# Layer 0 of the first two pairs entirely as squares of sums, and state copies by TensorE at the start

## What is computed

```python
e = stack([tbl_f[ids[:, f]] for f in range(32)], axis=1)      # 1024 x 32 x 16
x0, xk, outs = e, e, []
for W in (W0, W1, W2):                                        # W0 32x32x64, W1 and W2 32x64x64
    xk = relu(einsum('bmd,bhd,mhk->bkd', x0, xk, W))
    outs.append(sum(xk, axis=2))
h = concatenate([concatenate(outs, axis=1), dense_ctx], axis=1)
h = maximum(h @ W_top1 + b_top1, 0)
h = maximum(h @ W_top2 + b_top2, 0)
y = h @ W_top3
```

## Time and profile before

| | |
|---|---|
| median of 3 runs | 651.24 us (650.84 to 652.83) |
| the profiled execution | 651.33 us, its span 649.5 us |
| TensorE busy | 593.5 us (91%) |
| VectorE busy | 542.6 us (84%) |
| GpSimd busy | 441.0 us (68%) |
| ScalarE busy | 399.5 us (62%) |

### The profile page before, as it was taken

One profiled execution on the slowest core, in us unless ns is written; L12 is line 12 of the kernel. 1 busy time (PEld: TensorE's weight loads), 2 busy tenths in 40 slices (PEclk: granted clock), 3 DMA queues, 4 the chain that ended last, 5 costly groups with the idle time before them and its releaser, 6 DMA issues.

```text
span 649.5 us, 7363 instructions
## 1 busy us (share of the span) xinstructions
PE 593.5 (91%) x2580; PEld 187.3 (29%) x2580; DVE 542.6 (84%) x292; ACT 399.5 (62%) x644; POOL 441.0 (68%) x303
## 2 busy tenths in 40 slices
PE   0158699799999999999999999999999999999897
PEld 0012122233332333333333333333333333322243
DVE  0039889799899998989898989898999989899700
ACT  0041554967676777858586767676767778666032
POOL 5737766678897788889898988885989842522000
PEclk9998799999999999999999999999999999999999
DMA  3296989897978786959596968687877869030000
GB/s 102 70 248 145 225 190 235 205 221 194 216 197 193 207 181 182 207 157 214 144 213 169 196 168 200 150 213 149 211 167 197 179 188 194 32 64 0 9 9 0
DMA packets 41671, 104.57 MB, mean 161 GB/s; under 512 B 16897, under 2 KB 25665, under 8 KB 33442
## 3 DMA queue, kind: packets, MB, share of 16 engines
q1 hardware_dynamic: 32562, 100.53, 64.5%
q0 software_dynamic: 8192, 2.11, 3.6%
q10 hardware_dynamic: 880, 1.46, 0.8%
HBM read 99.08 MB, written 4.20 MB: 159 GB/s over the span
## 4 chain that ended last, share of the span: by engine, by line
PE 77%; DMA 7%; DVE 5%; issue 4%; POOL 4%; SPq 2%; ACT 1%; DVEq 0%
PE acc L531 59%; PE pair_sum L503 4%; DVE prod L330 4%; POOL gath L256 4%; PE pair_sum L518 4%; PE pair_sum L511 3%; DMA x_scratch<-gath 3%; PE pair_sum L524 2%; PE rep L589 2%; DMA gath<-in_tables,rows_sb 2%; DMA x_rot<-x_scratch 1%; SPq L231 1%; PE rep L581 1%; PE rep L582 1%; DVE z_sb L335 0%
## 5 line engine op out<-in xcount | busy, mean ns | idle before, releaser
L330 DVE TENSOR_TENSOR prod<-m_rep,rep 128x2048 f32<-128x2048 f32 x227 | 503.1, 2281 | 15.5 <-PE acc L531 11.2
L531 PE MATMUL acc<-prod,w_sb 128*64 128x512 f32 x1816 | 410.5, 601 | 18.4 <-DVE prod L330 16.5
L418 ACT COPY rep<-state 32x512 f32<-32x512 f32 x504 | 292.6, 581 | 52.2 <-DVE prod L330 45.3
L256 POOL DMA_INDIRECT gath<-in_tables,rows_sb x256 | 244.2, 954 | 94.8 <-issue 77.5
L531 PEld LDWEIGHTS acc<-prod,w_sb 128*64 128x64 f32 x1816 | 126.1, 138 | 295.9 <-issue 254.8
L267 POOL TENSOR_TENSOR prod_pool<-m_rep,xb 128x2048 f32<-128x2048 f32 x29 | 132.6, 4571 | 50.2 <-ACT xb L428 34.3
L267 POOL TENSOR_TENSOR prod_pool<-x_rot,x_rep 128x2048 f32<-128x2048 f32 x14 | 64.0, 4572 | 12.0 <-DMA x_rot<-x_scratch 9.0
L503 PE MATMUL pair_sum<-x0c,sel_sb 32*128 32x512 f32 x128 | 38.0, 670 | 26.7 <-DMA x0c<-x_scratch 25.5
L390 ACT ACTIVATE state<-pair_sum 128x512 f32<-128x512 f32 x16 | 9.6, 597 | 79.9 <-PE pair_sum L524 79.9
L531 PE MATMUL acc<-prod_pool,w_sb 128*64 128x512 f32 x232 | 54.7, 592 | 0.0
L411 ACT ACTIVATE sums_sq<-pair_sum 128x1024 f32<-128x1024 f32 x32 | 32.9, 1027 | 33.5 <-PE pair_sum L503 33.5
(11 more groups left out here) (27 smaller groups left out, 84.4 us busy)
## 6 DMA issues: line engine op xcount, KB each, us to landing
m_rep<-x_scratch SPq DMA_DIRECT2D x256, 256.0 KB, 9.4
x_rot<-x_scratch SPq DMA_DIRECT2D x32, 512.0 KB, 5.8
x_rep<-x_scratch SPq DMA_DIRECT2D x16, 512.0 KB, 3.8
gath<-in_tables,rows_sb POOLq DMA_INDIRECT x256
x_scratch<-gath SPq DMA_DIRECT2D x16, 256.0 KB
x0c<-x_scratch SPq DMA_DIRECT2D x32, 64.0 KB
w_sb<-in_w ACTq DMA_DIRECT2D x2, 512.0 KB, 4.6
m_rep<-z_sb SPq DMA_DIRECT2D x12, 64.0 KB, 2.3
```

The costliest lines, as they stand in the source:

```text
L256: pool.indirect_dma_start(out=gath[p % 2][:, g, :], out_offset=None, in_=tables, in_offset=bass.IndirectOffsetOnAxis(ap=rows_sb[:, n:n + 1 ...
L330: nc.vector.tensor_tensor(prod[:, number % RING], in0, in1[:, None, :].to_broadcast([128, 2, PAIR]), ALU.mult).then_inc(unit_ready, 1)
L418: last = nc.scalar.copy(rep[v][M * q:M * q + M, CHUNK * a:CHUNK * a + CHUNK], state[l - 1][K * a + M * v:K * a + M * v + M, :])
L531: last = nc.tensor.matmul(acc[K * a:K * a + K, :], w, src[:, k, CHUNK * a:CHUNK * a + CHUNK], start=start and k == 0, stop=stop and k == 1)
```

## The change

For pairs 0 and 1 (`EARLY = 2`) all four tiles of layer 0 are squares of sums, with the weights of tiles 0 and 1 halved (`half_sb`) and a diagonal of their own (`wdiag0_sb`). So `x_rep` and `x_rot` are not loaded for them, and the scratch is written once instead of twice. The gathered rows of a pair now lie as four blocks of 32 partitions, one for each quarter of the columns. Pair 0's sums are made straight from them by 16 matmuls of 256 columns, two pair-sum tiles at a time into eight PSUM half-tiles; pair 1's `x0c` is copied from them within the chip. TensorE runs five extra matmuls (`WARM`) once 10 gathers have landed. For slots 0 and 1, `rep[0]` of slot 2 and `rep[0]` of slot 3, the state is copied by matmuls with a 0/1 matrix (`copy_state`). Slot 0 takes its units in the order (0,0) (1,0) (0,1) (1,1) ... , which uses `m_rep` tiles as they land. On GpSimd `layer0_product(2)` comes after seven fours of gathers instead of eight.

```diff
 def order(i):
     if i == 0:
-        return [(0, 0), (0, 1), (1, 0), (1, 1), (0, 2), (1, 2), (0, 3), (1, 3)]
+        return [(v, u) for u in range(4) for v in range(2)]
...
 # SyncE, for p in range(NP)
-                sp.wait_ge(gathered[p % 2], 16 * GPP * (p // 2 + 1))
-                dst = x0_dram[p].rearrange("(again m) c -> again (m c)", again=2).rearrange("again (r c) -> r again c", c=PAIR // Q)
-                src = gath[p % 2][:, :, :].rearrange("r g d -> r (g d)")
-                sp.dma_start(dst, src[:, None, :].to_broadcast([128, 2, PAIR // Q])).then_inc(x0_stored, 16)
-                sp.wait_ge(x0_stored, 16 * (p + 1))
-                after(sp, l0_done, p - 1)
-                for a in range(2):
...
+                gathered_all(sp, p)
+                rows = gath[p % 2][:, :, :].rearrange("r g d -> r (g d)")
+                if p == 1:
+                    for q in range(Q):
+                        at = M * (q // 2), PAIR // Q * (q % 2)
+                        sp.dma_start(x0c[1][at[0]:at[0] + M, at[1]:at[1] + PAIR // Q],
+                                     rows[M * q:M * q + M, :]).then_inc(x0c_in[1], 16)
+                for again in range(1 if p < EARLY else 2):
+                    row = x0_dram[p, M * again:M * again + 1, :]
+                    dst = bass.AP(row.tensor, row.offset, [[PAIR // Q, Q], [PAIR, M], [1, PAIR // Q]])
+                    sp.dma_start(dst, rows).then_inc(x0_stored, 16)
+                sp.wait_ge(x0_stored, x0_stored_to(p + 1))
+                if p > 1:
+                    after(sp, l0_done, p - 1)
+                    for a in range(2):
+                        sp.dma_start(x0c[p % 2][M * a:M * a + M, :],
+                                     x0_dram[p, 0:M, CHUNK * a:CHUNK * a + CHUNK]).then_inc(x0c_in[p % 2], 16)
+                if p >= EARLY:
...
 # GpSimd
-            for n in range(8):
+            for n in range(7):
                 pool.wait_ge(unit_ready, 2 * n + 1)
                 gather(2 * GPP + 4 * n, 4)
             layer0_product(2)
-            for n in range(8, 10):
+            for n in range(7, 10):
...
 # VectorE
+            nc.vector.tensor_scalar(half_sb, w0_sb[:, 0:XT, :], 0.5, None, ALU.mult)
...
-            def first_layer0(p):
-                dve.wait_ge(x_in, 16 * (1 + XT) * (p + 1))
-                nc.vector.tensor_tensor(prod_pool[:, p], x_rot[:, :, :], x_rep[:, None, :].to_broadcast([128, XT, PAIR]),
-                                        ALU.mult).then_inc(first_x, 1)
...
-            def second_chunk(l):
...
 # ScalarE
-            square_x(0)
-            square(0, 0)
-            square(0, 1)
+            gathered_all(act, 0)
+            nc.scalar.activation(xsq[:, 0:PAIR // Q], gath[0][:, :, :].rearrange("r g d -> r (g d)"), SQUARE).then_inc(xsq_ready, 1)
+            act.wait_ge(first_sums, 1)
+            for half, sums in enumerate((pair_sum, rep[0])):
+                nc.scalar.activation(first_squares(0, half), by_block(sums), SQUARE).then_inc(first_sq, 1)
+            act.wait_ge(first_sums, 2)
+            nc.scalar.activation(first_squares(1, 0), by_block(rep[1]), SQUARE).then_inc(first_sq, 1)
+            for b, bank in enumerate((acc1, acc2)):
+                nc.scalar.activation(first_squares(1, 1)[:, b], bank[:, :].rearrange("p (t c) -> p t c", t=2),
+                                     SQUARE).then_inc(first_sq, 1)
             relu0(0)
-            replicate(0, 0, 1)
-            replicate(0, 1)
             relu_slot(0)
...
-                    square(i, 0)
-                    square(i, 1)
+                    for n in range(ST if i < EARLY else QB):
+                        square(i, n)
...
 # TensorE
+            def first_pair_sums():
+                gathered_all(pe, 0)
...
+                for sel_of, banks in ((sel0_sb, (pair_sum[:, 0:CHUNK], pair_sum[:, CHUNK:PAIR], rep[0][:, 0:CHUNK], rep[0][:, CHUNK:PAIR])),
+                                      (sel_sb, (rep[1][:, 0:CHUNK], rep[1][:, CHUNK:PAIR], acc1[:, :], acc2[:, :]))):
+                    for t in range(2):
+                        for q in range(Q):
+                            last = nc.tensor.matmul(banks[q][:, c * t:c * t + c], sel_of[M * q:M * q + M, t, :],
+                                                    rows[M * q:M * q + M, :], start=True, stop=True)
+                    last.then_inc(first_sums, 1)
...
+            def first_layer0():
+                pe.wait_ge(xsq_ready, 1)
+                pe.wait_ge(first_sq, 2)
+                layer0_tile(half_sb[:, 0, :], prod_pool[:, 0, 0, :], True, False)
+                first_diagonal(0)
+                layer0_tile(half_sb[:, 1, :], prod_pool[:, 0, 1, :], False, False)
+                first_diagonal(1)
+                pe.wait_ge(first_sq, 5)
+                for t in range(QB):
+                    last = layer0_tile(w0_sb[:, XT + t, :], sums_sq[:, t, :], False, t == QB - 1)
+                last.then_inc(l0_done, 1)
...
+            def copy_state(i, v):
+                l = SLOTS[i][0] - 1
+                pe.wait_ge(state_ready[l], SLOTS[i][1] + 1)
+                if i > 0:
+                    pe.wait_ge(unit_ready, UNIT_BASE[i] if i == 1 else UNIT_BASE[i - 1] + v0_units(i - 1))
+                for a in range(2):
+                    last = nc.tensor.matmul(rep[v][:, CHUNK * a:CHUNK * a + CHUNK], copies_sb[K * a:K * a + K, v, :],
+                                            state[l][K * a:K * a + K, :], start=True, stop=True)
+                last.then_inc(rep1_ready if v else rep0_ready, 1)
...
+            pe.wait_ge(first_gathered, 16 * WARM_FROM)
+            for _ in range(WARM):
+                nc.tensor.matmul(acc2[0:K, :], w_sb[1][:, 0, 0, :], w_sb[1][:, 0, :, :].rearrange("p t k -> p (t k)"),
+                                 start=True, stop=True)
+            first_pair_sums()
+            first_layer0()
+            copy_state(0, 0)
+            copy_state(0, 1)
...
+                    if i == 0 and n == 7:
+                        copy_state(1, 0)
+                        pair_sums(1, 0)
+                        copy_state(1, 1)
+                        pair_sums(1, 1)
+                    if i == 1 and n < 2:
+                        pair_sums(1, 2 + n)
+                    if i == 1 and n == 2:
+                        layer0_sums(1)
+                        layer0_rest(1)
+                    if i == 1 and n == 3:
+                        copy_state(2, 0)
...
+                    if (i, n) == (2, 3):
+                        layer0_sums(2)
+                    if (i, n) == (2, 4):
+                        layer0_rest(2)
+                    if (i, n) == (2, 5):
+                        copy_state(3, 0)
```

More of the change, by code:

```diff
@@ L211, in _ @@
-                for a in range(2):
[L212 to L215, removed]
-                rows = x0_dram[p, 0:1, :]
-                src = bass.AP(rows.tensor, rows.offset, [[PAIR, M], [0, Q], [1, PAIR]])
-                sp.dma_start(x_rep[:, :], src).then_inc(x_in, 16)
-                for t in range(XT):
-                    rows = x0_dram[p, 1 + Q * t:2 + Q * t, :]
-                    src = bass.AP(rows.tensor, rows.offset, [[PAIR, M], [PAIR, Q], [1, PAIR]])
-                    sp.dma_start(x_rot[:, t, :], src).then_inc(x_in, 16)
+                gathered_all(sp, p)
@@ new lines, in _ @@
+                sp.wait_ge(x0_stored, x0_stored_to(p + 1))
[5 more added lines that the diff above has]
+                if p >= EARLY:
+                    if p > EARLY:
+                        x_multiplied(sp, p - 1)
+                    row = x0_dram[p, 0:1, :]
+                    src = bass.AP(row.tensor, row.offset, [[PAIR, M], [0, Q], [1, PAIR]])
+                    sp.dma_start(x_rep[:, :], src).then_inc(x_in, 16)
+                    for t in range(XT):
+                        row = x0_dram[p, 1 + Q * t:2 + Q * t, :]
+                        src = bass.AP(row.tensor, row.offset, [[PAIR, M], [PAIR, Q], [1, PAIR]])
+                        sp.dma_start(x_rot[:, t, :], src).then_inc(x_in, 16)
@@ L336, in sum_d @@
                                         op=ALU.add, axis=AX_X).then_inc(z_ready[l], 1)
-            def second_chunk(l):
-                dve.wait_ge(state_ready[l], 1)
-                for q in range(Q):
-                    last = nc.vector.tensor_copy(rep[0][M * q:M * q + M, CHUNK:PAIR], state[l][K:K + M, :])
-                last.then_inc(first_rep, 1)
-                dve.wait_ge(first_rep, l + 1)
-            first_layer0(0)
             for i, (l, p) in enumerate(SLOTS):
                 base, nv = UNIT_BASE[i], v0_units(i)
-                if i < 2:
-                    second_chunk(i)
                 if i >= POOL_FROM:
@@ new lines, in layer0_tile, with first_diagonal @@
+            def layer0_tile(w, src, start, stop):
+                for a in range(2):
+                    last = nc.tensor.matmul(acc0[K * a:K * a + K, :], w, src[:, CHUNK * a:CHUNK * a + CHUNK],
```

(12 more changed lines are left out.)

178 lines of the change are left out of this document (105 added, 73 removed).

## The result

The changed kernel takes 649.93 us (median of 18 runs, 648.03 to 651.92), the kernel before 652.26 (18 runs, 650.45 to 654.36). The ratio is 0.9962, interval 0.9948 to 0.9976; the medians are 2.3 us apart. I had predicted 638.4 and a range that begins at 634.5 and ends at 643.5. The sign was right and most of the gain is missing. The profiled execution after has a span of 648.9 us against 649.5.

What follows compares the result with a forecast made beforehand. TensorE's own work bounds the middle, and a chain of DMA stages sets when it begins. That chain ends 12.9 us earlier (123.28 to 110.4), the engines' chain being ready at 108.0: 651.3 - 12.9 = 638.4 us, range 634.5 to 643.5.

Steps and rivals of the forecast that it cites:

- the DMA chain: Start, gathers, stores and loads of pairs 0 to 3: sets when the middle begins; 12.9 us earlier.
- 108.0: Engines' chain: TensorE ready for slot 3's pair sums at 108.0, 2.4 us before the data.
- taken two at a time: Pair 0's narrow matmuls: two overlap, so eight take 2.5 us; 1.3 if four overlap.
- 110.4: Slot 3's pair sums: start at 110.4 instead of 123.28, 2.3 us after x0c of pair 3 is issued.
- this moved step: GpSimd, pair 3's last four gathers behind layer0_product(2): landed at 103, at worst 106.5; costs nothing to 0.6 us.
- 2.15 us is nearly all latency: Pair 0's store, half as large: lands at 28.1 as before, no gain counted.
- The second store issue: Pair 2's stage: its 0.4 us is hidden, since the store waits behind the loads.
- my 51.2: Pair 1's gathers: the last lands at 51.2 instead of 58.3, bounds 46 and 53.
- the four `x0c` copies: Pair 1's stage on SyncE: four small issues before the store, 1.7 us in all.
- The next interval: From pair 1's stage at 55.1 to x0c of pair 2 at 78.8: 23.7 us instead of 31.2.
- I count full clock: TensorE in the start: no wait above about 2.3 us; otherwise 2 to 4 us more on the engines' chain.
- Rival A: Start: gathers land promptly, engines set the end at 108.0; 15.3 us less, 636.0 us; chance 0.14.
- Rival D: GpSimd: layer0_product(2), waiting for x_rot, delays pair 3's gathers; harm from x_rot at about 106, 655 at 110; chance 0.02.

Runs made afterwards that it cites:

- `f_best` paced: Changed kernel with pair 3's last gathers before GpSimd's product, stores as four DMAs, pair 1's store before its x0c copies, and pacing: 642.08 us (0.9860).
- the paced one: Changed kernel with SyncE waiting for each set of four m_rep loads before issuing the fourth of the next: 648.64 us (0.9957).
- The three mends: In the changed kernel: pair 3's last gathers before GpSimd's product, stores as four DMAs, pair 1's store before its x0c copies; paced 642.08 us against 648.64.
- pacing: SyncE waits for each set of four m_rep loads before issuing the fourth of the next; in the kernel before: 652.28 us (1.0006).
- `f_best`: The three mends in the changed kernel, without pacing: 677.14 us (1.0023), later 677.03 (1.0022), both on chips with stalls.

## Why the prediction was wrong

**What held.** The bound is the DMA chain, as forecast: TensorE's last wait before the middle is for `x0c` of pair 3, and the middle keeps its periods. In the view of waits, TensorE's waits for `x0c` up to 124 us went from 25.5 us in two to 7.8 in one. VectorE's first product is at 37.10 (37.0 forecast), slot 0's RELU at 59.22 (57.3), TensorE ready for slot 3's sums at 112.8 (108.0): 4.8 us late, but still ahead of the data. The sixteen narrow matmuls go from 26.23 to 28.24, so four of them do overlap, where I had taken two at a time. Layer 0 ends at 35.1 all the same, as forecast.

**What failed.** Sums of slot 3 at 120.65 and not 110.4, and 2.0 us of slow clock behind it: 12.3 us in the profiled execution, 11.5 in the medians. By size it is the store 4.2 us (3.0 for pair 3, 1.2 for pair 1), pair 3's gathers 2.5, the clock 2.0, pair 1's gathers 1.3, its four copies 0.85, and 1.25 without a cause. By its terms, from the trace of the changed kernel:

1. *"So this moved step costs nothing to 0.6 us"* is the step that let the last interval grow. I had the last gathers issued by 98.9 and landed at 103. The last was issued from 104.65 to 105.6, because `x0c` of pair 2 was 4.6 us late already and `x_rot` came 12.8 us after it and not 10.5, and then took 8.4 us, near my own worst case of 8.9. By my reckoning the store had to be issued by 27.1 us after `x0c` of pair 2 (78.8 to 105.9), which is 110.5 in this trace. It was issued at 113.05, 2.5 later, and then took 5.2 us to `x0c` and not 2.2, another 3.0 (term 2). Together that is the 5.5 us of the last interval. I had judged three margins one by one (when `x0c` of pair 2 comes, when `x_rot` comes after it, how long a gather lands), each at its likeliest value, and counted them as if only one could fail; they stand on one chain with one sign and add up.
2. *"2.15 us is nearly all latency, so I count nothing for it"*: a single store took 3.4 us and a double one 5.2, against 2.2. The change gives the store's target an outermost dimension of 4. The Trainium skill, "DMA: Bandwidth & Descriptors" (Why a DMA increments its semaphore by 16 and not by 1), says that the number of engines on a transfer is the largest k up to 16 that divides the slowest dimension on both sides, so here 4. The trace agrees: share 0.22 to 0.35 with those stores alone in SyncE's queue, and 0.57 to 0.61 for pair 3's store when that dimension is 32.
3. *"The second store issue (0.4 us) is hidden, since the store waits behind the loads"*: that cover was gone as soon as term 1 made the store late. With it went the cover of pair 3's 3.0 us of term 2.
4. Pair 1: gathers landed 1.3 us after my 51.2 (half of it a slip: 3 gathers in 4.5 us make 5.2 for 3.5, and I had added 4.6); the four `x0c` copies took 2.55 us of SyncE and not 1.7; the store 1.2 more. Together 3.4. The next interval lost 1.25 more, which no run explains.
5. *"I count full clock"* rested on a wait of at most 2.3 us. From slot 3's sums to the end the span needs 526.2 us in the kernel before and in `f_best` paced, 528.3 and 528.8 in the changed kernel and the paced one, whose waits were 7.80 and 4.84. So a wait of 1.61 or 1.90 us cost nothing behind it, and of the two long ones the shorter cost more. The clock is a term of its own that follows from terms 1 to 4.

Rival A had gathers landing promptly; the last ones took 8.3 and 8.4 us, so it is out again. A part of that is the gathers just ahead in GpSimd's own queue, which I had not kept apart from SyncE's loads. Rival D named the right mechanism, the product ahead of the gathers, and put its turning point too late: it took `x_rot` at 106 for harm to begin. `x_rot` came at 96.2 and it did harm, since against the data of a kernel that is 13 us earlier, and not against the kernel before, each microsecond of it counts.

**How far the runs carry this.** That the store of pair 3 waited for the gathers behind the product, and when, is shown by SyncE's wait and the chain of the changed kernel. What each term costs is read from that one trace; no run took away the gathers' delay alone, or the store's alone, on a chip without stalls. The three mends together, with pacing in both kernels, give 6.6 us there. In the traces 2.7 us of it come before `x0c` of pair 2 and 2.6 from the clock; 0.5 are lost again between `x0c` of pair 3 and the sums. The mended gathers show no gain there, because pacing had already brought them in time. Without pacing the interval in which they were late was 34.81 us, with it 30.94, so the 5.5 us of the last interval is no price of the gathers alone. Nor is it the price in every execution: the changed kernel's times spread over 3.9 us, and the paced one's trace is from the fastest of twelve. `f_best` without pacing was not timed on such a chip, so whether pacing has a part in 642.08 stays open. None of the three traces has the 29.3 of the kernel before; 1.6 us of the two paced ones are unexplained. What makes ScalarE and VectorE stall is open. On chips where they do, the kernel before takes 20 to 24 us more and the changed kernel, in the one comparison of it there, 27; the change gains nothing there (ratio 1.0007).

## What to carry to other kernels

When a chain of stages is shortened, ask of every step beside it how much slack it has against the new chain, and add up the likely misses of one sign instead of taking them as alternatives. An instruction that waits on an in-order engine holds back all the DMAs queued behind it: issue first what others wait for. When a store gets a new layout, look at its slowest dimension on both sides before calling its time latency.

## What the hardware did that I had not expected

The same kernel's time differs between chips by more than anything that the change does: in the six groups of runs, on five chips or six (that of the result is not named), the kernel before takes 652 us in two and 672.7 to 675.4 in the other four. In the traces of those four, all of the changed kernel and its edits, ScalarE stands idle 10.3 to 11.3 us before one and the same instruction, and VectorE at times up to 12.4, with nothing that the profile shows to wait for. Four 32-row matmuls of 256 columns share the array at once: each lasts 0.38 to 0.48 us, and sixteen take 2.0 us in all. The last gather of pair 0 takes 2.3 us to land, with SyncE's queue empty; the last ones of pairs 1 and 3 take 8.3 and 8.4 beside its loads, and 5.5 in the paced kernel (101.52 to 106.99), so the landing goes with how much stands in the other queue, and in part with the gathers ahead in its own.
